# A Hadamard transform of weights, from a program of its own into the first two chunks of a selective-scan kernel

## The reference

```
x  = fwht(x * SU_ug) / 64
up = x @ W_up.T * (Wscale_ug[:2048] * 64);  gate = x @ W_gate.T * (Wscale_ug[2048:] * 64)
x  = fwht(silu(gate) * up * SU_dp) / 64
x  = x @ W_down.T * (Wscale_dp * 64)
```

## Time and profile before

| what | us |
|---|---|
| median of 3 runs | 2864.34 |
| lowest, highest | 2860.25, 2867.99 |
| the profiled execution | 2862.8 |
| its span, first to last instruction | 2861.0 |
| TensorE busy | 2522.2 (88%) |
| VectorE busy | 2279.4 (80%) |
| GpSimd busy | 2085.8 (73%) |
| ScalarE busy | 1821.8 (64%) |

### The profile page before, as it was taken

The page is one execution under the profiler, slowest core; times in us unless marked ns, Lnnn a source line. Parts: engine busy times, 40 slices in busy tenths (PEclk is TensorE's granted clock), DMA queues, the critical chain, the costliest instruction groups (busy, mean ns, idle before and its releaser), DMA issues.

```text
span 2861.0 us, 45756 instructions
## 1 busy us (share of the span) xinstructions
PE 2522.2 (88%) x15760; PEld 2155.7 (75%) x15760; DVE 2279.4 (80%) x2584; ACT 1821.8 (64%) x3936; POOL 2085.8 (73%) x1714
## 2 busy tenths in 40 slices
PE   1546676999999999999999999999999999989987
PEld 0234555888888888888888888888888888877776
DVE  7817898888889888888888888988888989889321
ACT  0347776777767777767676776767676777755221
POOL 6228787878878797879787887878786978777221
PEclk8876998999999999999999999999999999999999
DMA  5651112565666666666656666666566565656586
GB/s 210 256 186 52 54 54 89 203 222 199 224 209 221 216 207 213 221 205 209 223 197 226 209 218 212 216 216 213 206 219 216 197 220 206 210 183 226 206 307 245
DMA packets 163879, 573.83 MB, mean 201 GB/s; under 512 B 17472, under 2 KB 19904, under 8 KB 129856
## 3 DMA queue, kind: packets, MB, share of 16 engines
q1 hardware_dynamic: 163648, 570.90, 58.0%
HBM read 536.75 MB, written 34.08 MB: 200 GB/s over the span
## 4 chain that ended last, share of the span: by engine, by line
PE 51%; DVE 22%; ACT 7%; POOL 5%; issue 5%; DMA 2%; DVEq 0%; POOLq 0%; ACTq 0%; SPq 0%
PE pF L652 15%; DVE h L999 11%; PE pM L597 10%; PE hT L584 9%; DVE acc L1010 7%; PE pD L665 7%; PE pM L634 7%; POOL dbx L1131 3%; DMA wug<-scratch_ug 2%; POOL conv L1187 2%; PE decay L652 1%; ACT L832 1%; PE hT L576 1%; ACT decay L832 1%; ACT delta L814 1%
## 5 line engine op out<-in xcount | busy, mean ns | idle before, releaser
L999 DVE TENSOR_TENSOR_SCAN h<-decay,dbx 128x512 f32<-128x512 f32 x1024 | 1203.2, 1207 | 294.0 <-ACT decay L832 237.0
L1131 POOL TENSOR_TENSOR dbx<-u,bb 128x2048 f32<-128x2048 f32 (+1 forms) x272 | 1177.8, 4331 | 81.0 <-DVE h L999 79.5
L832 ACT ACTIVATE decay<-delta,a_neg 128x255 f32<-128x255 f32 x2048 | 870.4, 467 | 207.4 <-DVE h L999 202.2
L652 PE MATMUL pF<-fxT_hi,wug 128*128 128x256 f32 x3840 | 749.4, 288 | 8.2 <-DMA wug<-scratch_ug 6.1
L584 PE MATMUL hT<-ident,h 128*128 128x128 f32 x4096 | 551.9, 279 | 130.3 <-DVE acc L1010 111.0
L584 PEld LDWEIGHTS hT<-ident,h 128*128 128x128 f32 x4096 | 481.0, 144 | 242.1 <-issue 160.2
L1010 DVE SCALAR_TENSOR_TENSOR acc<-hT,bcT,acc 128x1024 f32<-128x1024 f32 x480 | 606.6, 1264 | 34.8 <-PE hT L584 33.1
L652 PEld LDWEIGHTS pF<-fxT_hi,wug 128*128 128x128 f32 x3840 | 615.8, 192 | 11.5 <-DMA wug<-scratch_ug 8.9
L652 PE MATMUL pF<-fxT_lo,wug 128*128 128x256 f32 x1920 | 543.8, 283 | 0.0
L597 PE MATMUL pM<-xnT,w_in 128*128 128x256 f32 x2048 | 491.5, 384 | 10.9 <-ACT hid L773 3.4
L597 PEld LDWEIGHTS pM<-xnT,w_in 128*128 128x128 f32 x2048 | 375.5, 193 | 55.7 <-ACT hid L773 5.4
(11 more groups left out here) (113 smaller groups left out, 2511.3 us busy)
## 6 DMA issues: line engine op xcount, KB each, us to landing
wug<-scratch_ug SPq DMA_DIRECT2D x256, 1024.0 KB, 4.8
wd<-scratch_wd SPq DMA_DIRECT2D x256, 512.0 KB, 4.1
w_in<-in_W_in SPq DMA_DIRECT2D x256, 256.0 KB, 2.9
bb<-scratch_bc SPq DMA_DIRECT2D x128, 256.0 KB, 4.8
scratch_ug<-split_hi SPq DMA_DIRECT2D x8, 1024.0 KB, 5.9
scratch_ug<-split_lo SPq DMA_DIRECT2D x8, 1024.0 KB, 6.8
xb<-in_hidden_states SPq DMA_DIRECT2D x16, 512.0 KB, 4.9
xr<-in_hidden_states SPq DMA_DIRECT2D x16, 512.0 KB, 5.6
```

The lines of the kernel that those rows point to most:

```text
L652: mm = pe.matmul(gate_up_bank(no)[:, which, :], wug[no % 2][:, 2 * which + a, kt, :], fxT[b][:, kt, :], start=(kt == 0 and i == 0), stop=( ...
L832: e = act.activation(da[q % 2][:, i, 1:], delta[c % 2][:, dt, 1:], ACT.Exp, scale=a_neg[:, dt, n:n + 1])
L999: dve.tensor_tensor_scan(row(h[n % 2][:, tiles, :]), row(da[q % 2][:, :, :]), row(dbx[n % 2][:, tiles, :]), 0.0, ALU.mult, ALU.add).then_i ...
L1131: pool.tensor_tensor(dbx[n % 2][:, tiles, :], u[:, tiles, :], rows, ALU.mult).then_inc(done if restarts(c) else prod_done, 1)
```

## The change

- **hadamard_block is gone**; its work is in `fused_block`, whose memory is laid out anew so that the buffers of the transform lie where w_out, h, acc, gate, xr and the weights' buffers of the feed-forward part lie later. New waits guard each first use of such a place.
- **Up and gate are transformed wholly on TensorE**: each of 32 output tiles is four matmuls, with h128 or its negative, summed in PSUM. There are no butterflies for them.
- **W_down** keeps its butterflies, now in front0, first multiplied by Wscale_dp (`scale_down`). VectorE takes 352 of the 512 columns, GpSimd 160, each on its own. 16 matmuls follow.
- **Where the matmuls stand**: 16 (the outputs 0 to 3 of the first group) in front0, the first 8 ahead of x_proj, the others behind dt_proj. The rest is spread over the ends of the slots of steps 0 and 1; ScalarE's `had_high` and VectorE's `had_low` of an output stand in the slot after its last matmul, the stores one later. Three banks (pF and the two pD) hold the outputs.
- **The convolution of chunk 0** moves from ScalarE and GpSimd to VectorE (`conv_first`), between the butterflies.
- **The rounding** (`high`) moves from the even to the next odd slot, in all chunks.
- w_out is loaded in slot 28 of step 0; the load of `ones` was unused and goes.

```diff
-def hadamard_block(nc, W, scratch_ug, scratch_wd):
...
+        GROUPS = [("up", 0)] + [("down", q) for q in range(KT)] + [("up", q) for q in range(1, KT)] + [("gate", q) for q in range(KT)]
+        NTILE = KT * len(GROUPS)
...
+        SETS = ["x" if g % 2 == 0 else "y" for g in range(8)] + ["r"] * (len(GROUPS) - 8)
+        had_bank = [t[:, :, :].rearrange("p a t -> p (a t)") for t in (pF,)] + [t[:, :] for t in pD]
...
+        HAD_EVAC[0, 0] += [2]
+        HAD_EVAC[0, 1] += [3]
+        HAD_STORE[0, 2] += [0]
+        HAD_LOAD[0, 1] += UG_GROUPS[1:2]
+        todo = [(o, i) for o in range(KT, NTILE) for i in range(steps_of(o))]
+        for c in range(2):
+            for k in range(SLOTS):
+                room = (1 + k % 2 if k < 11 else 4 if k < 16 else 2) if c == 0 else 2
+                while room and todo:
+                    o, i = todo.pop(0)
+                    HAD_PE[c, k].append((o, i))
+                    room -= 1
+                    if i == steps_of(o) - 1:
+                        at = divmod(SLOTS * c + k + 1, SLOTS)
+                        HAD_EVAC[at].append(o)
+                        if o % KT == KT - 1:
+                            HAD_STORE[divmod(SLOTS * c + k + 2, SLOTS)].append(o // KT)
+                            HAD_LOAD[at] += UG_GROUPS[2:4] if o // KT == KT else next_in(o // KT) if o // KT in UG_GROUPS else []
+        DVE_COLS = 352
+
+        def scale_down(eng, i, cols, done):
+            tiles = slice(TILES // 2 * i, TILES // 2 * (i + 1))
+            eng.wait_ge(down_in[i], 16)
+            eng.wait_ge(wscale_in, 16)
+            eng.tensor_tensor(w_down[:, tiles, cols], w_down[:, tiles, cols],
+                              wscale[:, :, cols].broadcast_to([P, TILES // 2, cols.stop - cols.start]), ALU.mult).then_inc(done, 1)
+
+        def butterfly(eng, i, stride, cols, done, count):
...
+            eng.wait_ge(done, count)
+            eng.tensor_tensor(d0, s0, s1, ALU.add).then_inc(done, 1)
+            eng.tensor_tensor(d1, s0, s1, ALU.subtract).then_inc(done, 1)
...
@@ SyncE: load_ug, load_wd, load_res, front0 @@
+                if no == 0:
+                    for part in ("r_hi", "r_lo"):
+                        wait_first(sp, had_stored[part], 16 * SETS.count("r"), sp_passed)
...
+                if no == 0:
+                    wait_first(sp, had_mm, NTILE, sp_passed)
...
+                if j == 0:
+                    wait_first(sp, had_stored["y_lo"], 16 * SETS.count("y"), sp_passed)
...
                 load_pieces("hid", 0, 0)
                 load_pieces("hid", 0, 1)
+                sp.dma_start(wscale[:, :, :], W["Wscale_dp"].rearrange("(a b n) -> a b n", a=1, b=1).broadcast_to([P, 1, DM])).then_inc(wscale_in, 16)
+                load_down(0)
...
+                load_pieces("hid", 0, 2)
                 load_x(1)
-                load_pieces("hid", 0, 2)
+                load_down(1)
                 load_pieces("hid", 0, 3)
+                load_had(0)
                 load_pieces("hid", 1, 0)
-                sp.dma_start(w_out[:, :, :], W["W_out"].rearrange("(k p) n -> p k n", p=P)).then_inc(loaded_late, 16)
...
@@ TensorE @@
+            def had(o, i):
+                g, r = divmod(o, KT)
+                if i == 0:
...
+                    if o >= len(had_bank):
+                        pe.wait_ge(had_lo, o - len(had_bank) + 1)
+                    if g in UG_GROUPS and r == 0:
+                        pe.wait_ge(had_loaded[IN_BUF[g]], 16 * (in_use(g) + 1))
+                if g in UG_GROUPS:
+                    src, last, minus = had_in[IN_BUF[g]][:, i, :], i == KT - 1, (r & i).bit_count() % 2
+                else:
+                    src, last, minus = w_down[:, KT * GROUPS[g][1] + r, :], True, 0
+                mm = pe.matmul(had_bank[o % len(had_bank)], h128[minus][:, :], src, start=(i == 0), stop=last)
...
@@ ScalarE: had_high, gates, slot @@
+            def had_high(o):
+                g, r = divmod(o, KT)
+                act.wait_ge(had_mm, o + 1)
...
+                if r == 0 and split_use(g):
+                    act.wait_ge(had_stored[f"{SETS[g]}_hi"], 16 * split_use(g))
+                act.activation(split_row("hi", o), bank_tiles(o), ACT.Copy, scale=had_scale(o)).then_inc(had_hi, 1)
...
-                if k >= 4 and k % 2 == 0 and ff is not None:
-                    high(ff, (k - 4) // 2)
+                if k >= 5 and k % 2 and ff is not None:
+                    high(ff, (k - 5) // 2)
...
@@ VectorE: conv_first, front0 @@
+                for dt in tiles:
+                    dve.tensor_scalar(conv[0][:, dt, :], hid[:, dt, HALO:], taps[:, dt, HALO:HALO + 1], b_conv[:, dt:dt + 1],
+                                      ALU.mult, ALU.add).then_inc(first_tap, 1)
+                for k in range(HALO):
+                    for a, dt in enumerate(tiles):
...
+                        dve.scalar_tensor_tensor(conv[0][:, dt, :], hid[:, dt, k:k + T], taps[:, dt, k:k + 1], conv[0][:, dt, :],
+                                                 ALU.mult, ALU.add).then_inc(tap_added, 1)
...
+                mine = slice(0, DVE_COLS)
+                scale_down(dve, 0, mine, turned_dve)
+                conv_first(0)
+                butterfly(dve, 0, 1, mine, turned_dve, 1)
+                conv_first(1)
+                butterfly(dve, 0, 2, mine, turned_dve, 3)
                 x_stats(1)
+                conv_first(2)
+                butterfly(dve, 0, 4, mine, turned_dve, 5)
+                conv_first(3)
+                scale_down(dve, 1, mine, turned_dve)
+                for i, stride in enumerate((1, 2, 4)):
+                    butterfly(dve, 1, stride, mine, turned_dve, 8 + 2 * i)
+                dve.wait_ge(had_setup, 5)
+                for o in range(2):
+                    had_low(o)
+                butterfly(dve, None, 8, mine, turned_dve, 14)
...
@@ GpSimd: front0 @@
-                for dt in range(DT):
-                    add_taps(0, dt)
+                theirs = slice(DVE_COLS, DM)
+                for i in range(2):
+                    scale_down(pool, i, theirs, turned_pool)
+                    for at, stride in enumerate((1, 2, 4)):
+                        butterfly(pool, i, stride, theirs, turned_pool, 7 * i + 1 + 2 * at)
+                    if i == 0:
+                        moments("x", 1)
+                butterfly(pool, None, 8, theirs, turned_pool, 14)
+                pool.wait_ge(tap_added, HALO * DT)
                 halo(1)
-                moments("x", 1)
```

More of the change, by code:

```diff
@@ L233, in sem @@
             return ctx.enter_context(nc.semaphore(name))
+        wug = [sb(f"wug{i}", [P, 4, KT, P], F32R) for i in range(2)]
+        wd = [sb(f"wd{i}", [P, 2, DM], F32R) for i in range(2)]
+        fxT = [sb(f"fxT_{s}", [P, KT, T], F32R) for s in ("hi", "lo")]
+        fo = sb("fo", [P, TB, DM])
+        th = sb("th", [P, T])
+        prod = [sb(f"prod{i}", [P, T]) for i in range(2)]
+        prod_hi = [sb(f"prod_hi{i}", [P, T], F32R) for i in range(2)]
+        prod_lo = [sb(f"prod_lo{i}", [P, T], F32R) for i in range(2)]
+        xr = [sb(f"xr{i}", [P, TB, DM]) for i in range(2)]
+        acc = {1: sb("acc1", [P, TB, DI])}
+        w_out = sb("w_out", [P, DT, DM])
+        h = [sb(f"h{i}", [P, DT, T]) for i in range(2)]
+        acc[0] = sb("acc0", [P, TB, DI])
+        gate = sb("gate", [P, DT, T])
         w_x = sb("w_x", [P, DT, DTR + 2 * NST])
         w_dt = sb("w_dt", [P, DI])
-        w_out = sb("w_out", [P, DT, DM])
         RING = 4
@@ new lines, in split_use, with in_use, next_in, split_row @@
+        def split_use(g):
+            return SETS[:g].count(SETS[g])
+        IN_BUF = dict(zip(UG_GROUPS, (0, 0, 1, 2, 0, 1, 2, 0)))
+        def in_use(g):
+            return [IN_BUF[i] for i in UG_GROUPS if i < g].count(IN_BUF[g])
+        def next_in(g):
+            return [i for i in UG_GROUPS if i > g and IN_BUF[i] == IN_BUF[g]][:1]
+        def split_row(s, o):
+            g, r = divmod(o, KT)
+            t = split[f"{SETS[g]}_{s}"]
+            return t[:, r, :].rearrange("p (a m) -> p a m", a=KT) if GROUPS[g][0] == "down" else t[:, :, :].rearrange("p a (k m) -> p k a m", k=KT)[:, r, :, :]
@@ new lines, in bank_tiles, with had_scale @@
+        def bank_tiles(o):
+            return had_bank[o % len(had_bank)].rearrange("p (a m) -> p a m", a=KT)
+        def had_scale(o):
+            g, r = divmod(o, KT)
+            return row_scale[:, KT * GROUPS[g][1] + r:KT * GROUPS[g][1] + r + 1] if GROUPS[g][0] == "down" else su_ug[:, r:r + 1]
+        HAD_PE, HAD_EVAC, HAD_STORE, HAD_LOAD = ({(c, k): [] for c in range(2) for k in range(SLOTS)} for i in range(4))
+        steps_of = lambda o: 1 if GROUPS[o // KT][0] == "down" else KT
+        HAD_EVAC[0, 0] += [2]
@@ L507, in slot @@
                         b_rows(front, 1)
+                for g in HAD_STORE.get((c, k), ()):
+                    store_had(g)
+                for g in HAD_LOAD.get((c, k), ()):
+                    load_had(g)
```

(9 more changed lines are left out.)

309 lines of the change are left out of this document (124 added, 185 removed).

## The result

The changed kernel takes 2763.01 us (median of 4 runs, 2760.57 to 2769.74) against 2864.32 (2860.25 to 2867.99): ratio 0.965, 95% interval 0.9629 to 0.9672. The forecast was 2743 in a range of 2705 to 2790. The profiled execution took 2760.57, its span is 2758.8.

The account below looks back on a forecast made before the run. VectorE was taken to pace chunks 0 and 1, TensorE to bound the middle chunks. 2862.8 - 124 (start) + 18 + 11 (chunks 0, 1) + 2 (chunk 2's start) - 28 (rounding) = 2741.8, stated as 2743 us, range 2705 to 2790.

Parts of the forecast that it names:

- The start: Before the first scan: scan at 100 us, between 104 if VectorE and GpSimd alternate and 93; gain 124 us.
- Contention of the taps: In the front, GpSimd also blocks the convolution's multiply-adds on VectorE: chain ends at 104 us, without it near 93.
- Behind the last projection: In the front, eight Hadamard matmuls (6.9 us) behind the last dt projection mostly fill TensorE's idle time: +2 us.
- Chunk 0: First chunk: added Hadamard work, summed by slots with the larger of VectorE and TensorE, gives 145 us, +18.
- Chunk 1: Second chunk: the same sum by slots, 139 us, plus 11 of stalls gives 150 us, +11.
- The rounding: Chunks 2 to 15: rounding a slot later frees 2.0 us of TensorE's waiting per chunk, -28 us (0 to -45).
- Rival 1: The rounding gives nothing, since GpSimd takes the wait over: 2771 us, chance 0.20.
- Rival 2: Queues of chunks 0 and 1 couple, TensorE waiting for a low part two outputs back: +55, 2775 us, chance 0.15.
- my own case: The forecast itself, 2743 us, with chunks 0 and 1 together +29: chance 0.49.
- Rival 3: Better start without contention of the taps (92), and rounding worth 3.0 us per chunk: 2721 us, chance 0.13.
- Rival 4: TensorE stays at 1.2 GHz in chunks 0 and 1, waiting for VectorE each slot: +273, 3016 us, chance 0.03.

Follow-up runs that it names:

- dve_all: The changed kernel with all 512 columns of W_down's scaling and butterflies on VectorE, none on GpSimd: 2748.03 us, ratio 0.9591.
- low_twice: The changed kernel with 29 low parts (outputs 2 to 30) computed a second time by VectorE, into unused memory: 2782.2 us, ratio 0.97.
- best2: best1 with the Hadamard matmuls of a slot also moved right behind the turn of h, as in mm_first: 2738.72 us, ratio 0.9555.
- before_round: The kernel before the change with only the rounding moved to the odd slots: 2840.39 us, ratio 0.9912.
- round_back: The changed kernel with the rounding put back in the even slots: 2792.11 us, ratio 0.9745.
- thin_mm: The changed kernel with the Hadamard matmuls of chunks 0 and 1 over 64 of 512 columns: 2751.46 us, ratio 0.9593.
- best1: dve_all with three of four up and gate evacuations a slot later, chunk 0's convolution earlier and Hadamard output 2 ahead of x_proj: 2741.3 us, ratio 0.956.
- taps_back: dve_all with chunk 0's convolution back on ScalarE (products) and GpSimd (additions): 2761.86 us, ratio 0.964.
- mm_first: The changed kernel with a slot's Hadamard matmuls, from slot 4 on, right behind the turn of h: 2755.5 us, ratio 0.9619.

## Why the prediction was right, and where it wasn't

The direction and the places were right: the start gives nearly all, chunks 0 and 1 give some back, the rounding a little in each chunk. The sum was 19 us too good.

- **The start**: forecast 100 for the first scan, measured 103.40, gain 120.5 instead of 124, within 114 to 132. The chain was the one described, and half-stages of VectorE took 2.95 us beside GpSimd and 1.6 alone, as forecast. The last tap ended at 72.4 (73.1 in the alternating case), 31.0 us later came the scan (28.6 + 2 forecast). That the 73.1 fits so closely is in part luck: VectorE's first multiplication, which waits for W_down, began at 20.8 and not at 18.5, and what stands between it and the last tap took 51.6 us and not 54.6. I had taken 100 between two ends; 103.4 is near the end of alternation, 104, and far from the other, 93. But other kernels with the same front had the scan at 100.3 to 103.7 (last section), so the 3 us alone decide nothing between 100 and 104. The taps alone are 8 x 0.36 + 24 x 0.41 = 12.7 us (12.8 forecast).
- **Contention of the taps**, of which no row of before told: six multiply-adds take 2.46 us alone and up to 8.97 beside GpSimd. The rule cited from the Trainium skill ("SBUF — State Buffer", Who interferes with whom) holds here for the convolution as well; the rows agree for an addition, a multiply-add and a multiplication. By it the chain would end at 104, and it ended at 103.4. It also carried the forecast for dve_all (scan at 84, measured 85.31). An instruction with one large input and two scalars (L1065) was slowed too, 4.59 us for two instead of 0.72. The sentence cited is on instructions with two SBUF inputs and says nothing of this one; the figure stands as measured.
- **Behind the last projection**: the eight matmuls that now stand ahead of TensorE's turn of x for chunk 1 took from 92.4 to 100.4:

```profile
97.83 1.88 PE L647 MATMUL pF<-had_in,h_minus 128*128 128x512 f32 x4
...
100.41 1.04 PE L516 MATMUL hT<-ident,xb 128*128 128x128 f32 x8
```

  8.0 us against 6.9 in the forecast, and the scan waits for what follows the turn: ScalarE copies the turned x (to 102.5) ahead of the first decays, which release the scan. +2 was right.
- **Chunk 0**: 148.2 instead of 145. VectorE paces it, as forecast; low_twice shows that added busy time of VectorE costs 0.8 to 0.9 of itself.
- **Chunk 1: +11 forecast, +20.2 measured. This is the term that was mis-sized**, half of what is missing. The step was the addition of VectorE's and TensorE's loads by slots, and a remainder for stalls carried over from chunk 0. It had left out two waits of ScalarE that don't show in loads. One: the evacuation stands ahead of the next slot's decays, while its matmul stands at the end of TensorE's slot (8 waits for pD, 15.6 us). Two: the last four groups share one buffer, and one 1 MB store was waited for (4.30 us). The prediction put the new waits for reused memory at nothing and named w_out, acc and the residual; this buffer isn't in its list. With both waits gone (best2) chunk 1 took 149.3, where 150 had been forecast: the sum of the loads fits, the waits were what it lacked. How the 9.7 us divide between the two wasn't measured.
- **The start of chunk 2**: +2 forecast, nothing measured. Chunk 2 is 1.6 us shorter, like the others.
- **The rounding**: forecast 2.0 per chunk, measured 1.6. The mechanism was the one named: ScalarE's wait at the rounding is gone, VectorE idles 2.80 us behind the SiLU instead of 4.49 (near 2.5 forecast), and one of TensorE's three waits goes wholly. Of the others one falls from 1.13 to 0.65, and one stays at 1.19, where I had expected a part to go.
- **Rival 1** (the rounding gives nothing) falls by before_round and round_back. **Rival 2** (the queues couple, +55) lies about as near in size as my own case (+41.5, between +55 and +29), but not by its mechanism: TensorE waits 0.2 us for a low part in chunk 0, and for low parts it is three outputs back, not two as I wrote. The queues did couple, by ScalarE's waits in chunk 1. **Rival 3** falls: the taps were slowed. **Rival 4** (TensorE at 1.2 GHz): the granted clock is 0.99 and 0.98 in chunks 0 and 1, above the 0.82 and 0.91 of before. With more work TensorE got more clock, and thin_mm, with less, fell back to 0.82 and 0.89.

## What to carry to other kernels

Moving work under another stage costs what it puts on that stage's pacing queue, so price it there by the pacing engine, and then walk the order slot by slot: an evacuation early in one engine's slot of a matmul late in another's, or two uses of one buffer around a store, costs time that no sum of busy times shows. Splitting elementwise work over VectorE and GpSimd gained nothing here: giving it all to VectorE was 15 us faster, and in best1 work of GpSimd that came beside VectorE's butterflies took back what the shorter chain had won. A wait removed on a side engine is worth only what the bounding engine had waited because of it (16.7 us of ScalarE's wait gave 1.6).

## What the runs showed of the hardware

- VectorE and GpSimd hold each other up for more than two-input additions. GpSimd's multiplication by the scales, 1280 elements, at two places of the changed kernel, VectorE at work in both:

```profile
20.86 5.79 POOL L302 TENSOR_TENSOR had_down<-had_down,had_wscale 128x1280 f32<-128x1280 f32 x1 [13.15 <-DMA had_down<-in_W_down]
...
49.69 3.11 POOL L302 TENSOR_TENSOR had_down<-had_down,had_wscale 128x1280 f32<-128x1280 f32 x1
```

  At 20.82 VectorE began its own multiplication, which took 3.09 us, and GpSimd took 5.79. At 49.69 VectorE was in six multiply-adds of 256 elements, begun at 48.39: they took 6.36 us instead of 2.46, and GpSimd only 3.11. In taps_back GpSimd's 256-element additions took 2.06 us, and VectorE's 2048-element butterflies beside them 2.70 or 2.81 instead of 2.28. In all three places the engine with the shorter instructions lost more.
- The 1 MB store that chunk 1 waits for landed 9.4 us after its issue in the changed kernel and 11.4 in mm_first; the median of the four in this chunk is 4.3. It is the one that was issued 0.7 us behind a 1 MB load of W_gate (issued 280.13, landed 7.6 us later), which the other three have not; from 280.85 to 290.35 the DMA engines were busy 92% of the time. That the load is the cause fits this, and no run moved it away.
- The front of kernels that differ only in chunks 0 and 1 varied: first scans at 103.40, 101.59, 101.68, 100.31 and 103.66. Differences of 1 to 3 us there, from one profile each, aren't evidence for anything.
